# Layer 2: tile steps between the feed-forward products, next element's key products at the end of the body; with three tiles, steps two places later

## What is computed

```python
x = L0_attn_x                                       # (16, 256, 128)
xn = _layernorm(x, axis=-1)
s = _L0_attn_ref(xn, ...)                           # linear attention, 16 heads of 64
g = _silu(_L0_ffn_ref(xn, ...))                     # attention, then 8 experts, 2 of them per token
x = x + s * g
xn = _layernorm(x, axis=-1)
s = _L1_attn_ref(xn, ...)                           # gated linear attention in chunks of 64, then an FFN
g = _silu(_L1_ffn_ref(xn, ...))                     # 8 experts, the best one per token
x = x + s * g
```

```python
        q = l2_normalize(q)
        k = l2_normalize(k)                         # k = xn @ Wk: the "key products"
        ...
        x = x + o @ Wo
        h = layer_norm(x, ln2_w, ln2_b)
        x = x + jax.nn.gelu(h @ W1 + b1, approximate=False) @ W2 + b2
        return x
```

```python
        h = jax.nn.relu(jnp.einsum('btd,edh->beth', x, W1) + b1[None, :, None, :])
        y = jnp.einsum('beth,ehd->betd', h, W2) + b2[None, :, None, :]
```

## Time and profile before

| | |
|---|---|
| time, median of 3 runs | 2120.31 us (2119.42 to 2131.37) |
| the profiled execution | 2147.45 us, its span 2145.7 us |
| TensorE busy | 1774.0 us, 83% of the span |
| VectorE busy | 1277.2 us, 60% |
| ScalarE busy | 998.2 us, 47% |
| GpSimd busy | 216.0 us, 10% |
| TensorE's mean granted clock | 0.947 |
| the 16 C bodies | from 983 us to about 2012 us of the span |
| last tiles and outputs (F) | from about 2012 us to the end |

### The profile page before, as it was taken

One profiled execution on the slowest core, in us unless ns is written; L12 is line 12 of the kernel. 1 busy time (PEld: TensorE's weight loads), 2 busy tenths in 40 slices (PEclk: granted clock), 3 DMA queues, 4 the chain that ended last, 5 costly groups with the idle time before them and its releaser, 6 DMA issues.

```text
span 2145.7 us, 61336 instructions
## 1 busy us (share of the span) xinstructions
PE 1774.0 (83%) x23060; PEld 1275.5 (59%) x23060; DVE 1277.2 (60%) x3518; ACT 998.2 (47%) x2242; POOL 216.0 (10%) x235
## 2 busy tenths in 40 slices
PE   6999999987988889857888788887888888888652
PEld 4566566665665656635575556565666666766552
DVE  5676666675566566545465657575666566665312
ACT  2454444444454455434554455355544445555332
POOL 0000010000000000020110011001111100110122
PEclk9999999999999999979999999999999999999887
DMA  3222222221112211221212221120121111121473
GB/s 134 82 91 91 97 97 100 108 81 62 55 61 71 71 48 43 91 83 51 71 47 65 61 70 47 59 58 27 58 63 57 48 57 54 51 62 37 164 214 115
DMA packets 97603, 161.01 MB, mean 75 GB/s; under 512 B 14729, under 2 KB 66057, under 8 KB 94090
## 3 DMA queue, kind: packets, MB, share of 16 engines
q1 hardware_dynamic: 88170, 135.05, 19.2%
q0 software_dynamic: 9248, 23.17, 3.5%
HBM read 96.45 MB, written 61.69 MB: 74 GB/s over the span
## 4 chain that ended last, share of the span: by engine, by line
PE 58%; DVE 13%; issue 11%; ACT 9%; SPq 3%; DMA 2%; another core or an unknown queue 2%; POOL 1%; DVEq 0%; ACTq 0%; POOLq 0%
PE psum L920 5%; PE psum L799 3%; PE psum L777 3%; PE psum L990 3%; PE psum L1005 3%; PE psum L910 3%; PE psum L1224 3%; PE psum L1012 2%; PE psum L1115 2%; PE psum L808 2%; PE psum L1074 2%; PE psum L959 2%; PE psum L1088 2%; PE psum L1153 2%; PE psum L844 2%
## 5 line engine op out<-in xcount | busy, mean ns | idle before, releaser
L1454 ACT ACTIVATE pts<-psum 128x512 f32<-128x512 f32 x192 | 99.1, 603 | 173.9 <-PE psum L959 173.4
L1936 DVE TENSOR_REDUCE mneg<-psum 128x2 f32<-128x512 f32 (+1 forms) x192 | 119.1, 683 | 63.1 <-PE psum L939 35.2
L684 POOL DMA_INDIRECT rows<-h,recA x64 | 61.8, 965 | 871.7 <-DVE recA L1679 744.2
L799 PE MATMUL psum<-txT,wt 128*128 128x128 f32 x864 | 118.6, 281 | 2.4 <-ACT txT L1329 2.4
L808 PE MATMUL psum<-wt,tg 128*128 128x128 f32 x528 | 82.8, 289 | 43.2 <-DVE tg L1646 43.2
L920 PE MATMUL psum<-wa,xT_s 128*128 128x512 f32 x256 | 117.8, 604 | 0.0
L1074 PE MATMUL psum<-xT_s,wa 128*128 128x256 f32 x512 | 115.7, 379 | 0.0
L708 POOL DMA_INDIRECT rows<-xn,recC x32 | 33.4, 1043 | 804.5 <-DVE recC L2119 693.4
L799 PEld LDWEIGHTS psum<-txT,wt 128*128 128x128 f32 x864 | 108.4, 196 | 6.9 <-ACT txT L1329 4.1
L1074 PEld LDWEIGHTS psum<-xT_s,wa 128*128 128x128 f32 x512 | 96.1, 190 | 13.2 <-issue 0.8
L808 PEld LDWEIGHTS psum<-wt,tg 128*128 128x128 f32 x528 | 71.1, 200 | 47.2 <-DVE tg L1646 47.2
(11 more groups left out here) (276 smaller groups left out, 4330.4 us busy)
## 6 DMA issues: line engine op xcount, KB each, us to landing
wt<-in_wB SPq DMA_DIRECT2D x84, 384.0 KB, 3.0
outs<-pbd SPq DMA_DIRECT2D x16, 1024.0 KB, 7.0
wt<-in_wD SPq DMA_DIRECT2D x24, 578.0 KB, 3.4
wa<-in_wD SPq DMA_DIRECT2D x15, 578.0 KB, 3.6
tx<-rows SPq DMA_DIRECT2D x132, 64.0 KB, 3.1
outs<-ty SPq DMA_DIRECT2D x132, 64.0 KB, 1.6
rows<-pbd SPq DMA_DIRECT2D x64, 128.0 KB, 1.8
rows<-pbd SPq DMA_DIRECT2D x8, 1024.0 KB, 3.9
```

The source lines that it names most:

```text
L799: last = mm(bank(f"th{j}")[:, c * P:(c + 1) * P], view[s][:, c * P:(c + 1) * P], txT[:, s, :], start=True, stop=True)
L1454: af(pT[:, n, :], bank(f"e{n}"), ACT.Exp, scale=float(HD) ** -0.5).then_inc(*frees(f"e{n}"))
L1936: ins = v.tensor_reduce(mneg[:, int(n >= 4), col:col + hs], sc, AX.X, ALU.max, negate=True)
```

## The change

Three edits, made alike on TensorE, ScalarE, VectorE and in the list of bank uses.

1. The key products `lk` of the next element, with their squares on ScalarE and their copies on VectorE, move from right behind `f0`, `f1` to the very end of the body, behind step 7.
2. Steps 5 and 6 now stand between `f0`, `f1` and `w2` (before: `lk` and step 5); step 7 stands between `w2` and `lk`.
3. In bodies with three tiles every step does what it did two places earlier: tile work starts at step 2 and ends at step 6 (`tile_delay`).

```diff
+def tile_delay(stages):
+
+    return 2 if "D" in stages else 0
+
 def uses_in_order(stages):
...
     def tile_step(u):
         count = tiles_in(stages)[0]
-        if u < count:
+        u -= tile_delay(stages)
+        if 0 <= u < count:
             names.append(f"tx{u}")
...
         names += ["f0", "f1"]
+        tile_step(5)
+        tile_step(6)
+        names += ["w2"]
+        tile_step(7)
         first_qk("lk")
-        tile_step(5)
-        names += ["w2"]
-        tile_step(6)
-        tile_step(7)
...
                     last.then_inc(*fills(f"f{j}"))
-                if "P" in now["stages"]:
-                    products("lk", INNER)
                 tile_step(5)
+                tile_step(6)
                 pe.wait_ge(*read_out("f1"))
                 pe.wait_ge(*emptied("w2"))
...
                 last.then_inc(*fills("w2"))
-                tile_step(6)
                 tile_step(7)
+                if "P" in now["stages"]:
+                    products("lk", INNER)
...
                 act.preload_act_table_set("natural_log_exp_and_others")
-                first_k()
                 tile_step(5)
                 tile_step(6)
                 tile_step(7)
+                first_k()
...
                 decay_means(1)
-                keys_turned()
                 tile_step(5)
+                tile_step(6)
                 dve.wait_ge(*filled("w2"))
...
                 dve.sem_inc(*signals("recC_ready"))
-                tile_step(6)
                 tile_step(7)
+                keys_turned()
```

## The result

The changed kernel takes 2160.65 us (median of 4 runs, 2154.69 to 2166.16); measured beside it, the kernel before takes 2122.74 us. The ratio is 1.0141, 95% interval 1.0092 to 1.0191: slower, by 37.9 us, with 2146 forecast and 2168 as the upper bound. A second comparison, at another time, gave 1.0173 (1.0151 to 1.0196).

A forecast was written before the change was run, and what follows sets the result against it. TensorE, busy 83%, was taken to bound the kernel. Losses in the D bodies, CP body and last tiles outweighed the B turns' -16.8 us: +26.4 us, 1.0123, or 2146 us; likeliest range 2136 to 2160, outer 2124 to 2168.

The forecast's parts named there:

- B, order, five turns: B turns ending in a jump: `lk` at the end covers the jump, 2.2 us gained a turn.
- B, clock, five turns: B turns: clock stays up over the jump, 2.2 us gained a turn, less 1.05 for idle gaps ahead of `w2`.
- B, two bodies without a jump: B bodies followed by no jump: new order costs 0.9 us, clock 0.35 each, +2.5 us in all.
- CP body: Body without tiles: `w2` needs Gelu at once instead of behind `lk`, +2.1 us, once.
- D, order, seven bodies: D bodies: front -2.4 us, `f` later by 1.1, end +4.8; +3.5 a body, +24.2 in all.
- D, clock: D bodies: 2.7 us idle lowers the clock, 1.6 us at a chance of 0.75, seven times, +8.4 us.
- CD body and last tiles: CD body: `ty2` comes later, so the last tiles' first load starts 6.0 us later, +6.0 us.
- Rival 3: Jump not covered by `lk`: L1084 starts 4.3 us behind its end; about +70 us, 2190; chance 0.10.
- Rival 2: Front of the D bodies gives back nearly all of its 4.0 us; 2135 us; chance 0.10.
- Rivals 1 and 4: Clock stays up: 2132 us, chance 0.25; with dense stretches in D bodies also faster: 2095 to 2105, chance 0.05.

The follow-up runs named there:

- b_split: Kernel before with only the seven B bodies reordered behind `f`: two `lk`, steps 5 and 6, `w2`, step 7, last two `lk`; ratio 0.9940, second time 0.9942.
- before_again: The kernel before, unchanged, profiled a second time: five B turns with a jump 364.6 us, seven D bodies 419.5 us.
- after_again: The changed kernel, measured and profiled a second time; ratio 1.0173 to the kernel before.
- split_delay1: Kernel before with `lk` divided in the B bodies, and every tile step of three-tile bodies one place later under the old end order; ratio 0.9969.
- w2_first: The changed kernel with `w2` moved ahead of step 6 in the D bodies alone; ratio 1.0033 to the kernel before.
- delay_only: The kernel before with the third edit alone, tile steps of three-tile bodies two places later; ratio 1.0171.

## Why the prediction was right, and where its terms were off

| term | predicted, us | measured, us |
|---|---|---|
| B, order, five turns | -11.0 | at full clock -13, idle time -12 |
| B, clock, five turns | -5.8 | the other way: busy time +7 |
| B, two bodies without a jump | +2.5 | +1.8 |
| CP body | +2.1 | +0.1 |
| D, order, seven bodies | +24.2 | about +25 |
| D, clock | +8.4 | about +4 to +8; busy time +13 |
| CD body and last tiles | +6.0 | +2.2 |
| sum | +26.4 | +28.2 by stretches; medians +37.9 and +34.7 |

The direction and the D bodies, which make the loss, were forecast by the right mechanism. That the sum comes so near the +28.2 is in part luck: the B clock was off by 13 us, and the CP body, the D clock and the last tiles together by about 10 the other way.

**B, order: right at full clock.** Idle time of 1.6 and 1.2 us was forecast ahead of `th5` and `ty4`, and 1.59 and 0.85 were found; L1084 at 14.2 us after `f`, and its weight load came at 14.15 (1241.65 to 1255.80). From `f` to that load it is 16.5 us on average over the five turns of before and 14.9 after; the three turns at full clock have 13.95, which is 2.6 us less where 2.2 were forecast; in the other two `w2` ran at the lower clock. Rival 3 has fallen, since `lk` covers the jump.

**B, clock: wrong.** The step that failed is that the clock would stay up over the jump and stay up then, worth 2.2 us a turn, less 1.05. Its first half holds (the first window starts behind the jump, and answers to the earlier trace rows), its second doesn't: the low stretches went elsewhere, now into dense work, so that the clock cost 7.0 us of busy time over the five turns instead of giving 5.8 back. Three windows after, the first behind a jump, the second behind the scores and `la`, the third over the end of a body:

```profile
1256.00:1263.90 7.90, 7.66 (x68) 2.93 (x68) 2.17 (x7) 5.22 (x12) 0.00 (x0) 1.00 0.45 129
...
1070.50:1077.00 6.50, 6.50 (x120) 6.16 (x115) 6.18 (x11) 1.66 (x5) 0.00 (x0) 0.50 0.02 5
...
1104.50:1107.90 3.40, 3.04 (x14) 3.04 (x15) 1.55 (x5) 0.79 (x2) 0.00 (x0) 0.51 0.08 24
```

The waits of TensorE ahead of the second of them:

```profile
1061.42 2.28 PE L1159 MATMUL psum<-qt,reg 64*64 64x64 f32 x119 [0.42 <-DVE reg L2077]
1065.08 0.35 PE L1159 MATMUL psum<-qt,reg 64*64 64x64 f32 x9 [1.38 <-issue]
...
1069.08 0.45 PE L1174 MATMUL psum<-tri,big 64*64 64x64 f32 x11 [1.78 <-issue]
```

The page that the prediction cited (the Trainium skill, TensorE: Matmul & The Clock Gate, HAM oscillation) says that gaps between bursts put the clock back to half. The traces agree for the long gaps of before; as a means to forecast a turn it did not do, for in the changed kernel the clock fell at 1070 behind waits of 0.42, 1.38 and 1.78 us, and in b_split it stayed up for a whole turn behind a gap of 2.66. The prediction weighed single gaps against a bound between 1.87 and 2.12 us; no such bound exists in these traces. What decides was not found; that the same B work ran with 14 to 24, 30, or 34 to 60 us at the lower clock, depending on the order behind `f`, is measured.

**CP body: the end right, the sum wrong.** From `f` to the next body it is 9.45 us (1511.09 to 1520.54) against 7.28 in before_again, +2.2 with +2.1 forecast, but `f` starts 2.2 us earlier in the body (1.5 in after_again). Why the front is shorter was not followed up.

**D, order: right.** The bodies of after are compared with those of before_again, which lacks the same records. From the start of a body to `f` it is 49.3 us against 50.3 on average over the last six, -1.0, where -2.4 and +1.1 stood. In the first of the seven it is 48.85 against 55.03; this was in no term. From `f` on, the body shown takes 14.20 us against 8.98: +5.2, with +4.8 forecast; the wait for Relu is 2.35 (2.7), the bank of the last `lk` as described. One reading behind it was wrong: the gaps of 1.4 to 2.1 us at the end of the old D bodies were put down to the jump, of which queued work covers a part. They are in the main the wait for VectorE that split_delay1 shows, since the body that leaves the loop has it as well. The sum did not hang on it, as the forecast for the D bodies goes by the banks. Rival 2 has fallen. The front gave back what was expected: the scores wait 0.78 us for VectorE where there had been no wait, and `st` waits twice for nothing visible.

**D, clock: right in size, wrong in reason.** 20 to 31 us at the lower clock instead of 3 to 14, and TensorE's busy time about 13 us longer, of which a part falls into time in which it would have waited anyway. It was charged to the gap of 2.7 us, and w2_first, without that gap, has 7. But delay_only, whose longest gap in a D body is 2.23 us, has 54, so other gaps do it too. Rivals 1 and 4, in which the clock stays up, have fallen.

**Last tiles: the wait moved as forecast, and was mostly absorbed.** The first load of the last tiles, after (SyncE's queue), and TensorE at the first of them, before and after:

```profile
2025.56 0.35 SPq L572 DMA_DIRECT2D wa<-in_wD  x1
```

```profile
2011.91 0.33 PE L777 MATMUL psum<-ident,tx 128*128 128x128 f32 x1 [0.44 <-DMA tx<-rows]
```

```profile
2029.24 0.33 PE L782 MATMUL psum<-ident,tx 128*128 128x128 f32 x1 [4.86 <-DMA tx<-rows]
```

The load stands 54.55 us behind the start of the CD body; before it was 48.64 (2008.18 less 1959.54): 5.9 us later, with 6.0 forecast (before_again has 50.74, so there it is 3.8). TensorE stands 4.86 us for it instead of 0.44. But the rest grew by 1.3 us in this profile and by 2.2 on average: the term assumed that everything hangs on the first load, while most of the later waits for rows are there with or without it.

The stretches sum to +28.2 us (-5.2, +1.8, +0.1, +29.3, +2.2), and the medians moved by 35 to 38. The missing 6 to 10 us are not placed. The part ahead of the first C body varies by 24 us (961.2 to 985.1) with unchanged code, most of it between the groups, two of which ran on a chip of the same number, and was 4.4 us longer in after_again than in before_again; whether the change has a part in that is open.

## What to carry to other kernels

Work that is moved behind a chain of another engine (here Gelu, two table loads and Relu) costs the length of the chain, and the sum of such rows was good to a few tenths of a microsecond per body; put something without a wait, as `w2` here, between the chain and its user. A body that waits for nothing and one that waits are different cases: the same edit gained where six tiles and a jump left a hole and lost where three tiles had left none, so make such an edit by kind of body. Do not book a gain for TensorE's clock because one gap is closed; measure the low stretches over the whole turn, more than one profile each. And before a gap at the end of a loop's body is called the jump's, look at the turn that leaves the loop: in the B bodies its gap is gone, in the D bodies it stays.

## What the runs showed of the hardware

- A jump back in a loop can cost TensorE some microseconds. In B bodies, counted from the start of `ty5` to the weight load of the next turn's first product: 3.7 to 5.7 us at the ten jumps of before and before_again, where nothing stands behind `ty5`, and 0.4 to 0.5 us in the bodies without a jump. With `lk` behind `ty5` it is 4.5 to 5.5 us at the ten jumps of after and after_again and 3.7 to 3.8 us without a jump. So the start of the next turn hardly moves, and `lk` hides most of the jump's cost. The Trainium skill (Runtime: NRT & Kernel Launch, Instruction fetch mechanics) says that a taken branch whose target lies outside the prefetched pages stalls for its fetch; the gaps at the jumps agree with it, but no row shows the fetch itself.
- The same gap of 1.7 us at the end of a body can have another cause: in the D bodies of before_again the next body's product starts 0.05 to 0.14 us behind the VectorE instruction that empties its bank, in the six bodies that jump and in the one that does not.
- Where the granted clock falls to its lower level depends on more than the last gap: in the same five turns it was low for 14 to 60 us, by the order of the last 15 us of a body, and a gap of 2.66 us left it up in one turn where waits of 1.78 us and less preceded a fall in another.
